# One ring of seven score banks in place of three pairs, in a four-block attention and expert kernel

## The chip, the core and the metric

The kernel runs as one program on one core of a Trainium2 chip. The metric is the device time of one execution in microseconds. PE is TensorE's matmuls, PEld its weight loads, DVE VectorE, ACT ScalarE, POOL GpSimd, SP SyncE. PSUM has eight banks of 512 fp32 values a partition, and it is the memory that matmuls write and that DVE and ACT read.

## The reference, cut to what matters

```python
# x: 4 x 512 x 256, context: 4 x 1601 x 256
x = x + tanh(g_xattn[0]) * xattn0(layernorm(x), context)   # block 1: 16 heads of 64, softmax over 1601 keys, Wo
x = x + tanh(g_ffn[0]) * ffn0(layernorm(x))                # block 2: below
x = x + tanh(g_xattn[1]) * xattn1(context, context, layernorm(x), mask)   # block 3: 16 heads of 16, 1601 masked keys, w_out
x = x + tanh(g_ffn[1]) * ffn1(layernorm(x))                # block 4: below

def ffn0(x):      # block 2
    src = rmsnorm(x + gqa(x))               # 16 query heads of 16, 4 key heads, 512 keys
    return rmsnorm(src + moe(src))          # 8 experts, 2 for each token, at most 640 tokens an expert

def ffn1(x):      # block 4
    attn = attention(x)                     # 16 heads of 16, 512 keys
    return attn + sum(combine[e] * (x @ W[e] + b[e]) for e in range(8))   # the best two weights, softmax gate
```

## The kernel before, in words

**Units and order.** Python code plans the whole program as one list of units (`order`), and each engine issues its part of every unit in the order of that list, waiting on the counting semaphores of the others. A unit is a small step: a matmul group on PE and what reads its result on ACT, DVE or POOL. `build_order` (from line 332) has eight generators for the first half of the program and eight for the second. The strings `TURNS_1` and `TURNS_3` say, digit by digit, from which generator the next unit comes. `Pace` (from line 194) keeps estimated times for every unit while the list is made; it chooses which part of the PSUM ring a unit gets. The assignment is fixed before the program runs.

**PSUM.** `RING` is 3: the ring is three pairs of banks (six banks). The two other banks, `pv_a` and `pv_b`, hold sums of value products: `pv_a` for blocks 1 and 3, `pv_b` for blocks 2 and 4. Every unit that needs PSUM takes a whole pair, the small ones too. A tile of scores with four heads (`scoreb`) takes two pairs, one for each half.

**Block 1** (`wide_...`, generators 0 to 4 of the first half): for each of 4 batches and 8 pairs of heads it projects keys (`kproj`), queries (`qproj`) and values (`vproj`), takes row maxima of bf16 scores (`maxa`, 16 units, matmul L1149 and DVE reduce L1671), turns them into a row (`rowa`), makes 13 tiles of scores with the maxima subtracted (`scorea`, L1165 and L1168, exp on ACT L1450, sums on POOL L1554), multiplies by the values (`pva`, L1179), and ends in `suma` and `outa` (ACT copy L1463). **Block 2** (generators 5 to 7) runs beside it, batch by batch, one batch behind.

**Blocks 3 and 4** share the second half: generator 0 mixes expert rows back, 1 makes scores of block 3, 2 its value products, 3 its maxima, 4 to 7 the same and the experts for block 4. Block 3 has 4 batches x 4 groups of 4 heads; a group has 13 key tiles. Each score tile (`scoreb`, mask matmuls L1290, score matmuls L1294, two exps L1457) uses 32x32 tiles of PE: a head lies on 32 rows (a strip), and four column parts of a head run side by side. The maxima of a group (`max3`) are 32 units: 4 query tiles x 4 key chunks x 2 pairs of heads; each fills a pair with 401 columns for either head (L1246, eight matmuls) and DVE adds the mask and reduces each bank (L1699, two instructions). `pvb` is a value product of a tile (L1310), and `tailb` (ACT copy L1467) ends a group. In block 4 `projqk` makes queries and keys of a group (L1214, L1215), `v4` the values (L1232, L1233), `expert4` one expert's product (L1388, L1389, DVE L1933).

**How a score tile waits.** In the code before, the two halves are issued one after the other, and the second waits for its own pair:

```python
for first in (0, 2):
    if first:
        for lane, other in plan.second_free[unit]:
            past.wait_ge(*at(lane, *other))
    ...   # masks of heads first, first + 1, then their scores
    last.then_inc(tensor_done, 1)
```

**Norms.** `ln`, `rms1` and `rms2` are one unit each: DVE makes means of squares, ACT takes the root (L1407), and DVE waits for it and then scales (L1653, L1835, L1852).

## Time and profile before

| | us |
|---|---|
| median of the runs | 3425.99 |
| lowest and highest of 3 | 3425.68, 3433.13 |
| the profiled execution | 3398.36 |
| its span, first to last instruction | 3396.6 |
| PE busy in the span | 3242.2 (95%) |
| DVE busy | 1980.8 (58%) |
| ACT busy | 1446.3 (43%) |
| POOL busy | 955.0 (28%) |
| mean granted clock of PE | 0.971 |

Busy means that at least one instruction of the engine runs. For PE a matmul on one 32x32 tile of the array counts as one on all of it. Rows of the trace name the line of the kernel, the engine, the operation and the tiles it writes and reads; the bracket behind a row tells how long the engine was idle before it and what ended that. "issue" stands for time in which the engine waited for nothing that the profile shows. The 27.6 us between the profiled execution and the median are part of what differs from execution to execution.

### The profile page before, as it was taken

To read this page: it belongs to the slowest core of one execution; us is meant where nothing else is said; L and a number is where in the kernel's file an instruction comes from. 1 tells how busy PE (TensorE), PEld (TensorE's weight loads), DVE (VectorE), ACT (ScalarE), POOL (GpSimd) and SP (SyncE) were. 2 spreads that over 40 slices of the span, in tenths; PEclk is the share of its full clock that TensorE was granted. 3 is DMA by queue.
4 is the path that set the end of the run, shared out by engine and by line. 5 is a ranking of instruction groups with operands and counts; after the bars stand their busy time and mean duration, and the time that the engine had idled before them with its cause. 6 is when DMAs were issued, how large, how long until landed. Compare 5 with 4: busy or idle time off the path is not lost.

```text
span 3396.6 us, 71446 instructions
## 1 busy us (share of the span) xinstructions
PE 3242.2 (95%) x30986; PEld 1431.6 (42%) x31007; DVE 1980.8 (58%) x4289; ACT 1446.3 (43%) x1645; POOL 955.0 (28%) x469
## 2 busy tenths in 40 slices
PE   7999999999999999999997979899999999999999
PEld 3444444444434444444433753223333334343344
DVE  4444456554655546565575028677777777766446
ACT  3444344445434453344433212355454454545533
POOL 4655554654465445555400000100000000000000
PEclk9999999999999999999988999899999999999989
DMA  4000000000000000000021622565343444443300
GB/s 152 12 13 13 28 12 15 7 11 33 7 21 12 13 28 7 21 12 12 4 116 39 188 81 75 132 175 158 97 120 115 127 124 117 118 118 113 115 26 20
DMA packets 85306, 221.17 MB, mean 65 GB/s; under 512 B 18424, under 2 KB 39168, under 8 KB 84224
## 3 DMA queue, kind: packets, MB, share of 16 engines
q1 hardware_dynamic: 79616, 201.65, 19.5%
q0 software_dynamic: 5376, 14.95, 2.0%
q8 instruction: 244, 4.00, 0.5%
q14 instruction: 70, 0.57, 0.1%
HBM read 204.61 MB, written 18.48 MB: 66 GB/s over the span
## 4 chain that ended last, share of the span: by engine, by line
PE 84%; DVE 6%; ACT 4%; POOL 3%; issue 1%; DMA 1%; ACTq 0%; POOLq 0%; DVEq 0%
PE ring L1294 13%; PE pv L1179 10%; PE ring L1168 9%; PE pv L1310 9%; PE ring L1246 3%; PE ring L1149 3%; PE ring L1140 3%; PE ring L1126 3%; PE ring L1141 3%; PE ring L1165 3%; PE ring L1127 2%; PE ring L1290 2%; POOL wide L1554 2%; PE ring L1367 2%; PE ring L1348 2%; PE ring L1260 2%
## 5 line engine op out<-in xcount | busy, mean ns | idle before, releaser
L1554 POOL TENSOR_TENSOR wide<-wide 124x1024 f32<-124x1024 f32 (+1 forms) x341 | 803.9, 2358 | 180.2 <-ACT wide L1450 142.2
L1457 ACT ACTIVATE wide<-ring 128x1024 f32<-128x1024 f32 (+1 forms) x544 | 536.2, 1023 | 498.4 <-PE ring L1294 494.6
L1671 DVE TENSOR_REDUCE max_a<-ring 128x2 f32<-128x802 f32 x512 | 493.4, 991 | 395.9 <-PE ring L1149 395.5
L1450 ACT ACTIVATE wide<-ring 124x1024 f32<-124x1024 f32 (+1 forms) x416 | 425.3, 1026 | 438.1 <-PE ring L1168 385.0
L1294 PE MATMUL ring<-slim 32*32 32x512 f32 (+1 forms) x7040 | 522.9, 607 | 0.3 <-DVE slim L1724 0.2
L1699 DVE CUSTOM_DVE_ANT_0 rest<-ring,slim 128x401 bf16<-128x401 f32 x683 | 374.9, 576 | 106.0 <-PE ring L1246 71.1
L1168 PE MATMUL ring<-wide 64*124 64x512 f32 (+1 forms) x1664 | 424.7, 588 | 0.0
L1179 PE MATMUL pv<-wide 124*64 124x512 f32 (+1 forms) x1664 | 413.9, 613 | 8.2 <-ACT wide L1450 8.2
L1709 DVE TENSOR_REDUCE slim<-ring 128x2 f32<-128x1024 f32 x256 | 308.0, 1222 | 111.9 <-PE ring L1260 105.4
L1524 POOL DMA_DIRECT2D slim<-in_ctx_k x16 | 8.9, 558 | 968.5 <-PE ring L1246 920.2
L1551 POOL TENSOR_TENSOR wide<-wide 124x1024 f32<-124x1024 f32 x31 | 73.1, 2357 | 599.5 <-ACT wide L1450 586.2
L1699 DVE CUSTOM_DVE_ANT_0 slim<-ring,slim 128x401 bf16<-128x401 f32 x341 | 195.8, 574 | 59.1 <-PE ring L1246 46.8
L1310 PE MATMUL pv<-wide,slim 128*17 128x512 f32 (+1 forms) x1664 | 226.4, 617 | 0.0
L1294 PEld LDWEIGHTS ring<-slim 32*32 32x32 f32 (+2 forms) x7040 | 173.3, 110 | 114.6 <-issue 73.8
L1246 PE MATMUL ring<-slim 32*32 32x401 bf16 x4096 | 192.0, 347 | 21.4 <-ACT wide L1457 8.8
L1179 PEld LDWEIGHTS pv<-wide 124*64 124x64 f32 (+1 forms) x1664 | 99.0, 136 | 229.2 <-issue 201.4
L1168 PEld LDWEIGHTS ring<-wide 64*124 64x124 f32 (+1 forms) x1664 | 155.5, 183 | 73.0 <-issue 50.4
L1246 PEld LDWEIGHTS ring<-slim 32*32 32x32 bf16 x4096 | 59.8, 88 | 288.6 <-ACT wide L1457 152.1
L1165 PE MATMUL ring<-wide,select_b 64*128 64x512 bf16 x832 | 159.0, 379 | 8.1 <-ACT wide L1450 6.1
L1149 PE MATMUL ring<-wide 64*128 64x401 bf16 x1024 | 155.5, 337 | 9.7 <-DVE max_a L1671 4.7
L1290 PE MATMUL ring<-slim,ident_b 32*32 32x512 bf16 (+1 forms) x3264 | 154.0, 394 | 10.9 <-ACT wide L1457 8.2
L1140 PE MATMUL ring<-wide 128*124 128x128 f32 (+1 forms) x832 | 162.1, 276 | 0.4 <-DVE max_a L1671 0.4
(238 smaller groups left out, 3964.3 us busy)
## 6 DMA issues: line engine op xcount, KB each, us to landing
slim<-masks SPq DMA_DIRECT2D x832, 128.0 KB, 2.7
slim<-in_ctx_k SPq DMA_DIRECT2D x16, 800.5 KB, 4.6
wide<-in_w_pair SPq DMA_DIRECT2D x32, 384.0 KB, 3.0
wide<-in_w SPq DMA_DIRECT2D x16, 512.0 KB, 4.7
wide<-in_we SPq DMA_DIRECT2D x16, 512.0 KB, 3.7
slim<-in_ctx_v SPq DMA_DIRECT2D x16, 442.0 KB, 5.9
wide<-in_ctxT SPq DMA_DIRECT2D x4, 1601.0 KB, 6.8
slim<-in_ctx_k POOLq DMA_DIRECT2D x16, 400.2 KB, 4.8
```

The lines of the kernel that those rows point to most:

```text
L1140: pe.matmul(place, ctxT[:, 0, k0:k0 + kn], pair_weights(p)[:, 2, 0, :], start=True, stop=False)
L1168: last = pe.matmul(slot[0:kn, h * BANK:(h + 1) * BANK], keys_a[own, p % 2, k0:k0 + kn], queries_a[own, p % 2, :], start=False, stop=True)
L1179: last = pe.matmul(pv_a[64 * h:64 * h + 64, :], values_a[0:kn, p % 2, k, 64 * h:64 * h + 64], exps_a[0:kn, slot_of["scorea", b, p, k], h * ...
L1246: last = pe.matmul(slot[j * PAD:(j + 1) * PAD, i * BANK:i * BANK + CHUNK], queries_low(3, g)[own, q * P + j * PAD:q * P + (j + 1) * PAD], ...
L1294: last = pe.matmul(head_bank(unit, h)[c0:c0 + cn, :], key_columns(blk, g, k0)[own, c0:c0 + cn], queries_place(blk, g)[own, :], start=blk ! ...
L1310: last = pe.matmul(pv_of[blk][PAD * h:PAD * h + rows_h, :], value_columns(blk, g, k, kn, h), exps_tile(blk, b, g, k, h)[0:kn, :], start=k ...
L1450: sc.activation(exps_a[0:kn, slot_of[unit], :], slot[0:kn, :], ACT.Exp, scale=WIDE ** -0.5).then_inc(scalar_done, 1)
L1457: sc.activation((exps_2 if blk == 2 else exps_34)[0:kn, first + 2 * i:first + 2 * i + 2, :].rearrange("p h n -> p (h n)"), ring_t[0:kn, ba ...
L1554: po.tensor_tensor(sums[0:kn, :], sums[0:kn, :], view, ALU.add).then_inc(pool_done, 1)
L1671: ve.reduce_max(max_a[:, :, q, c], slot.rearrange("p (h n) -> p h n", h=2)[:, :, 0:CHUNK], AX.X).then_inc(vector_done, 1)
L1699: ve.tensor_tensor_reduce(out=max_junk[junk], in0=slot[:, i * BANK:i * BANK + CHUNK], in1=maskQ_sb[:, q, CTX_CHUNKS[c]:CTX_CHUNKS[c] + CHUNK],
L1709: ve.tensor_reduce(neg_cols[blk][:, q, 2 * hp * PAD:2 * hp * PAD + PAD + 1:PAD], slot.rearrange("p (h n) -> p h n", h=2), AX.X, ALU.max, n ...
```

## The change

- The ring is seven single banks (`RING = 7`), and only `pv_a` keeps a bank of its own. Units whose result fits in one bank (`qproj`, `rowa`, `suma`, `projk`, `v2`, `strip`, `low`, `rowb`, `gate2`, `ranks`, `gate4`, `turn_comb`) take one. Units of a pair take banks 0 and 1, 2 and 3, or 4 and 5; bank 6 is for single ones alone.
- A score tile with four heads takes two pairs and waits for all four banks at its start. All masks are issued first, then all scores; ACT is told after head 1 and after head 3.
- `max3` has 64 units of one head and one bank, four matmuls and one DVE instruction, in place of 32 of two. The mask that DVE adds is laid out by chunk, with 1604 columns in place of 1601.
- The value sums of blocks 2 and 4 take one bank of the ring from the first value tile of a group to its copy on ACT.
- `projqk`, `v4` and `expert4` are two units of one bank each.
- `ln`, `rms1` and `rms2` are split: `stats` or `squares` (DVE, then the root on ACT) and the scaling as a unit of its own, which can lie further on in the order. Each has its own place for the root.
- `Pace` keeps a time for each of PE's four strips of rows and for the issue, and both strings of turns are new: 3911 turns in place of 3323.

```diff
-RING = 3
+RING = 7
+        if step.slots in (2, 4):
+            pairs = sorted(range(0, RING - 1, 2), key=lambda i: max(self.ring[i:i + 2]))[:step.slots // 2]
+            self.picked = tuple(bank for i in pairs for bank in (i, i + 1))
+        elif step.slots == 1:
+            ready = [i for i in range(RING) if self.ring[i] <= at]
+            self.picked = (max(ready, key=lambda i: self.ring[i ^ 1] if i ^ 1 < RING else 1e9) if ready else min(range(RING), key=lambda i: self.ring[i]),)
...
-                for c in range(len(CTX_CHUNKS)):
-                    for hp in range(2):
-                        yield Step(0.17 if b or g else 0.8, (("ve", 1.12),), 1, (("low", b, g),), ("max3", b, g, q, hp, c),
+                for c, h in product(range(len(CTX_CHUNKS)), range(GROUP)):
+                    yield Step(0.18 if b or g else 0.5, (("ve", 0.525),), 1, (("low", b, g),), ("max3", b, g, q, h, c),
...
-            yield Step(3.5, (("ve", 1.7),), 1, (("bias4", b),), ("expert4", b, e))
+            for i in range(2):
+                yield Step(1.75, (("ve", 0.85),), 1, (("bias4", b),), ("expert4", b, e, i))
...
-        ring_t = ctx.enter_context(nc.psum_tensor("ring", [P, RING, 2 * BANK], F32))
-        pv_t = ctx.enter_context(nc.psum_tensor("pv", [P, 2, BANK], F32))
-        pv_a, pv_b = pv_t[:, 0, :], pv_t[:, 1, :]
+        ring_t = ctx.enter_context(nc.psum_tensor("ring", [P, RING, BANK], F32))
+        pv_a = ctx.enter_context(nc.psum_tensor("pv", [P, BANK], F32))[:, :]
...
-                    for first in (0, 2):
-                        if first:
-                            for lane, other in plan.second_free[unit]:
-                                past.wait_ge(*at(lane, *other))
-                        if blk == 3:
-                            for h, (c0, cn) in product(range(first, first + 2), parts):
...
+                    if blk == 3:
+                        for h, (c0, cn) in product(range(GROUP), parts):
+                            own = slice(PAD * h, PAD * h + cn)
+                            pe.matmul(ring_t[c0:c0 + cn, bank_of[unit][h], :], ident_b[own, own],
+                                      mask_places[n % MASK_PLACES][own, c0 // PAD, :], start=True, stop=False)
+                    for h, (c0, cn) in product(range(GROUP), parts):
+                        own = slice(PAD * h, PAD * (h + 1))
+                        last = pe.matmul(ring_t[c0:c0 + cn, bank_of[unit][h], :], key_columns(blk, g, k0)[own, c0:c0 + cn],
+                                         queries_place(blk, g)[own, :], start=blk != 3, stop=True)
+                        if h == 1 and c0 == parts[-1][0]:
+                            last.then_inc(tensor_done, 1)
+                    last.then_inc(tensor_done, 1)
...
-                if kind in ("ln", "rms1", "rms2"):
-                    past.wait_ge(vector_done, plan.end["vector", unit] - {"ln": QT, "rms1": QT, "rms2": 2 * QT}[kind])
-                    sc.activation(rstd[:, :], rstd[:, :], ACT.Sqrt).then_inc(scalar_done, 1)
+                if kind in ("stats", "squares"):
+                    past.wait_ge(*at("vector", *unit))
+                    sc.activation(root_of(unit), root_of(unit), ACT.Sqrt).then_inc(scalar_done, 1)
```

## Rows read from the trace of the kernel before

**Rows 1.** Table by stage: stretch; length, busy us of each engine; clock, DMA share, GB/s.

```profile
core 0: us, PE busy (x) PEld busy (x) DVE busy (x) ACT busy (x) POOL busy (x), PEclk, DMA share, GB/s
355.00:1730.00 1375.00, 1341.27 (x7515) 610.94 (x7514) 764.69 (x1037) 603.91 (x706) 698.52 (x306) 0.99 0.05 15
1730.00:1835.00 105.00, 93.12 (x477) 35.23 (x483) 69.82 (x138) 42.79 (x49) 7.71 (x8) 0.89 0.24 95
1835.00:2010.00 175.00, 158.74 (x709) 123.52 (x710) 27.86 (x67) 36.70 (x53) 8.81 (x10) 0.94 0.45 140
2010.00:2120.00 110.00, 85.22 (x1134) 29.42 (x1143) 81.42 (x291) 23.76 (x26) 15.88 (x17) 0.91 0.28 73
2120.00:3260.00 1140.00, 1105.59 (x18173) 411.63 (x18156) 785.47 (x2400) 560.05 (x598) 22.74 (x30) 0.97 0.44 122
3260.00:3396.60 136.60, 121.76 (x1199) 62.75 (x1201) 84.33 (x139) 41.13 (x49) 0.00 (x0) 0.93 0.06 20
```

**Rows 2.** Timeline, one cycle of block 3: start, length in us, engine, line, operation.

```profile
2280.76 0.40 PE L1290 MATMUL ring<-slim,ident_b 32*32 32x512 bf16 x8
...
2283.28 0.11 PEld L1246 LDWEIGHTS ring<-slim 32*32 32x32 bf16 x8 [0.68 <-ACT wide L1457]
2283.30 0.58 DVE L1699 CUSTOM_DVE_ANT_0 rest<-ring,slim 128x401 bf16<-128x401 f32 x1 [0.98 <-PE ring L1246]
...
2284.58 0.41 PE L1290 MATMUL ring<-slim,ident_b 32*32 32x512 bf16 x8
...
2284.81 1.04 PE L1294 MATMUL ring<-slim 32*32 32x512 f32 x16
...
2285.29 0.57 DVE L1699 CUSTOM_DVE_ANT_0 slim<-ring,slim 128x401 bf16<-128x401 f32 x1
2285.43 0.11 PEld L1290 LDWEIGHTS ring<-slim,ident_b 32*32 32x32 bf16 x8 [0.49 <-DVE max_b L1699]
...
2285.79 0.57 DVE L1699 CUSTOM_DVE_ANT_0 rest<-ring,slim 128x401 bf16<-128x401 f32 x1
2286.04 1.95 ACT L1457 ACTIVATE wide<-ring 128x1024 f32<-128x1024 f32 x2 [1.89 <-PE ring L1294]
...
2287.07 0.58 DVE L1699 CUSTOM_DVE_ANT_0 rest<-ring,slim 128x401 bf16<-128x401 f32 x1 [0.70 <-PE ring L1294]
...
2287.41 0.13 PEld L1310 LDWEIGHTS pv<-wide,slim 128*17 128x17 f32 x8 [0.18 <-issue]
2287.41 1.05 PE L1310 MATMUL pv<-wide,slim 128*17 128x512 f32 x8
...
2288.57 0.40 PE L1290 MATMUL ring<-slim,ident_b 32*32 32x512 bf16 x8
```

**Rows 3.** Timeline: a score tile of block 4 whose four banks were free.

```profile
2513.34 1.15 PE L1294 MATMUL ring<-wide 32*32 32x512 f32 x32
...
2514.54 1.94 ACT L1457 ACTIVATE wide<-ring 128x1024 f32<-128x1024 f32 x2 [1.40 <-PE ring L1294]
```

**Rows 4.** What ended PE's idle time before L1246 (two rows), L1290 (two rows).

```profile
  ACT wide L1457: 149.9, 202
  DVE max_b L1699: 67.0, 92
...
  DVE max_b L1699: 87.4, 152
  ACT wide L1457: 32.2, 37
```

**Rows 5.** Who waited for ACT's root L1407: us in total, times.

```profile
  DVE src L1653: 8.9, 8
  DVE src L1852: 7.5, 4
  DVE slim L1653: 5.6, 4
  DVE wide L1653: 4.3, 4
```

**Rows 6.** Timeline: ACT's copies that end a wide pair (L1463), a masked group (L1467).

```profile
123.98 0.60 ACT L1463 ACTIVATE raw_a<-pv 128x512 f32<-128x512 f32 x1 [1.87 <-PE pv L1179]
169.99 0.60 ACT L1463 ACTIVATE raw_a<-pv 128x512 f32<-128x512 f32 x1 [1.85 <-PE pv L1179]
...
2213.79 0.60 ACT L1467 ACTIVATE raw_a<-pv 128x512 f32<-128x512 f32 x1 [1.91 <-PE pv L1310]
2268.25 0.60 ACT L1467 ACTIVATE raw_a<-pv 128x512 f32<-128x512 f32 x1 [1.67 <-PE pv L1310]
2321.13 0.60 ACT L1467 ACTIVATE raw_a<-pv 128x512 f32<-128x512 f32 x1 [2.12 <-PE pv L1310]
```

**Rows 7.** The chain of work: two fp32 matmuls of an expert unit, start and length.

```profile
3258.24 0.43 PE ring L1389 x2
```

More of the change, by code:

```diff
@@ L44 @@
 DIVIDE = 0.13
+ISSUE = 0.05
 AHEAD = 0.5
@@ L180, with __init__ @@
+    "33533323133613325333653321771462412146212147442214741214217525656162521617226444474467447644774477447744457546"
+    "454645464446744457546454645464446744454474565464546447465756565766776"
 )
 class Step:
-    def __init__(self, pe=0.0, use=(), slots=0, needs=(), name=None, parts=(1, 1), first=None, second=0.0, mark=None, late=0.0):
+    def __init__(self, pe=0.0, use=(), slots=0, needs=(), name=None, parts=(1, 1), mark=None, late=0.0, rows=range(4), hold=0):
         self.pe, self.use, self.slots, self.needs, self.name = pe, use, slots, needs, name
-        self.parts, self.first, self.second, self.mark, self.late = parts, first, second, mark, late
+        self.parts, self.mark, self.late, self.rows, self.hold = parts, mark, late, tuple(rows), hold
@@ L208, in accept @@
+        at = max([at] + [self.ring[i] for i in self.picked])
         end = at
         if step.pe:
-            turned = self.pe + (DIVIDE if step.parts[0] != self.parts else 0.0)
-            at = max(at, turned)
-            if self.spare and at - self.pe >= WARM_FROM:
-                self.spare(at - self.pe)
-            end = at + step.pe
-            if step.slots == 2:
-                end += max(0.0, self.ring[self.picked[1]] - at - step.second)
-            self.pe, self.parts = end, step.parts[1]
+            if step.parts[0] != self.parts:
+                free = max(self.busy) + DIVIDE
+            else:
+                free = max(self.busy[r] for r in step.rows)
+            if self.spare and at - max(self.busy) >= WARM_FROM:
+                self.spare(at - max(self.busy))
+            self.issued = at + ISSUE
+            end = max(at, free) + step.pe
+            for r in range(4):
+                self.busy[r] = end if r in step.rows else max(self.busy[r], end - step.pe) if step.parts[0] != self.parts else self.busy[r]
+            self.pe, self.parts = max(self.busy), step.parts[1]
@@ L229, in accept @@
+            last = self.lane[lane] = max(self.lane[lane], ready) + time
+            if i == 0 or (i == 1 and step.slots == 4):
+                for bank in self.picked[2 * i:] if step.slots == 4 else self.picked:
+                    self.ring[bank] = last + HOP
+                if step.hold == 2:
+                    self.ring[self.held] = last + HOP
             if step.mark is None or i <= step.mark:
@@ L232, in accept @@
             for i in self.picked:
-                self.ring[i] = end + HOP
+                self.ring[i] = 1e9 if step.hold else end + HOP
+                self.held = i
         if step.name:
@@ L538, in slim_values @@
             also = (("outb", 3, b - 1),) if blk == 3 and b and last and g == 0 else (("bias4", b),) if blk == 4 and last else ()
[L539 to L541 removed]
+            own = blk != 3
+            yield Step(0.88, (("sc", 0.6), ("ve", 2.25 if g % 2 else 1.55)) if last else (), int(own and k == 0),
+                       (("scoreb", blk, b, g, k),) + valued + also, unit, (-4, -4), hold=int(own and k == 0) + 2 * int(own and last))
+            if own and k == 0:
+                in_slot(unit, "none")
+                bank, = plan.bank[unit]
+            emit(on(unit, *(() if own else pv_left)))
             expo.free[plan.slot["scoreb", blk, b, g, k]] = (("tensor", unit),)
```

429 lines of the change are left out of this document (221 added, 208 removed).

## The prediction

> **What bounds the kernel now.** I read the table by stage first [rows 1]. It cuts the span of 3396.6 us in seven: the wide attention (0 to about 1730), what is left of the grouped attention (to 1835), the expert layer (to 2010), the gathers (to 2120), a long stage in which masked attention and the last layer run together (2120 to 3260), and a tail. PE looks full everywhere: 1341 of 1375 us in the wide stage, 1106 of 1140 in the long one. In the wide stage this is nearly true work: of one pair of heads the copies of the sums stand 46.0 us apart [rows 6], and PE's idle time there is 33.7 us in 1375. In the long stage it is not, because a matmul on one 32-row strip counts as a busy PE though three other strips stand still. So I read one cycle of masked attention in the timeline [rows 2].
>
> There a score tile (`scoreb`) is issued in two halves. Masks and scores of heads 0 and 1 start at 2284.58, those of heads 2 and 3 at 2285.43, after a wait for DVE to leave the second pair of banks. Each half streams for 1.04 us on two strips only. Both exps follow in one run of 1.95 us from 2286.04. DVE takes six maxima, 0.50 us from start to start, and then stands still for 0.70 to 0.98 us until PE has new ones, which have no bank: the one pair left of the three is DVE's own, and PE's weight load waits until ACT has read another. The starts of three score tiles, 2280.76, 2284.58 and 2288.57, give a cycle of 3.9 us. DVE's work in it is 6 x 0.50 = 3.0 us, ACT's 1.95. PE's, if all four strips ran together as they do in a tile whose banks are all free (1.15 us, [rows 3]), would be 1.15 + 0.2 of masks + 1.05 of values + three double maxima of at most 0.17 stream each, about 2.9. Nobody is full; the three pairs of banks couple them. The waits by line say it for the stage [rows 4]: maxima wait for ACT's banks 149.9 us and for DVE's 67.0; masks wait for DVE's 87.4 and ACT's 32.2. Much of this lies under matmuls still running, so it is a sign and not a sum. The stage as a whole: DVE 785 and ACT 560 of 1140 us.
>
> **The change, part by part.** All on the profiled execution (3398.4 us with 1.8 around its span); the median of the runs is 3426.0, 27.6 above it, and I add that at the end.
>
> *Seven single banks; one-bank maxima; four-bank scores.* The masked maxima become 1024 units of one bank instead of 512 of a pair. Matmuls, reduce instructions and bytes stay the same; what is added is a wait and a signal for each, which costs nothing I can see, since DVE's two instructions of a unit already follow each other at the same 0.50 us as those of different units [rows 2]. A score tile takes two pairs and lets nothing start before all four banks are free. While it is in flight DVE has three banks, not two, and a bank comes back after each reduce. Work out the cycle: at 0 the masks start; the exps begin 1.46 later (2284.58 to 2286.04), say 1.5 with 16 mask loads ahead; they last 1.95; the bank goes over within 0.1. So the late pair of a score is free at 3.5. The next score can take that late pair and the pair it did not use, if the maxima in between sit in the single bank and in the early pair (free at 2.5). DVE needs 3.0 of these 3.5 us, PE 2.9. The cycle is then 3.5 instead of 3.9, bound by the two exps behind one score. There are 13 x 16 = 208 such tiles: 208 x 0.4 = 83 us. Against it: the accumulators of blocks 2 and 4 lose their own bank and hold one of the seven from the first value tile to the tail. With one bank gone the ring is three pairs again, and the cycle 3.9, as now. Block 4 holds one through much of the last three quarters of the stage. I take 60 of the 83; the bounds are 30 and 83. A check from other rows: with no block 4 beside it a group takes 54.5 and 52.9 us [rows 6]; 13 x 3.9 is 50.7 of that, so 13 x 3.5 makes it 48 to 49, and the same 8 to 10% on 1140 is 90 to 110. The bound is not reached there, as two engines would be at 80%; this leaves room below 60, not a forecast.
>
> *Splitting.* `projqk`, `v4` and `expert4` become two units each: 16 + 4 + 32 = 52 more. An expert unit is eight pairs of matmuls at 0.43 us, 3.4 us [rows 7], during which DVE has at most the work of the one pair in hand, about 1 us. Halved, PE can feed DVE in between. Per block this is worth from 0 to 1 us, 0 to 52 in all; I take 20, as DVE is behind in about a third of the stage. It is paid for by changes of PE's tile shape: the first weights of a value tile wait 0.18 us on "issue" after 32-row work [rows 2]. If each of the 52 extra units stands alone between masked work, that is two changes each, 52 x 2 x 0.18 = 19 us; I take 8. Net -12, from +19 to -52.
>
> On that change of shape TensorEngine Tiling (the Trainium skill, Key Properties) says that a change of tiling mode drains the engine while tiles within a mode run independently. The trace agrees with 0.18 us beside it. Taken in full the rule speaks against finer units, since a drain behind a score is its whole 1.15 us; by it the 52 units would cost up to 52 x 1.15 = 60 us, not 8.
>
> *Norms in two units.* The root of ACT comes between two DVE units, so DVE can go on instead of waiting for it. These waits are 8.9 + 7.5 + 5.6 + 4.3 us in the whole kernel [rows 5], 26.3; half of them lie where DVE is short. I take -8, from 0 to -26. The roots and the table loads stay as many. A split norm can also come later on its chain, which only the ends of stages would feel (up to 3 us each).
>
> *The wide stage.* Its tiles keep their pairs, and it is PE's own work that fills it. Smaller units (query projection, row sums, the single-bank steps of block 2) now leave the pairs alone. At most PE's 33.7 idle us and the staggered halves of block 2's 64 scores are to be had; those now need two free pairs at once, between wide scores that want them too. I take -15, from +15 to -50.
>
> *Ends.* Expert layer and gathers keep pairs, weights and DMAs: 0, within 3. The mask rows grow from 1601 to 1604 columns, nothing. In the tail (PE 121.8 of 136.6 us, [rows 1]) smaller expert units help DVE a little: -5, from +2 to -10.
>
> Sum: -60 - 12 - 8 - 15 - 5 = -100. 3398.4 - 100 = 3298; with the 27.6, **3326 us**.
>
> **Rivals.** *A, the wait moves ahead of the whole score.* Today the masks of the second half wait 119.6 us for DVE and ACT [rows 4] while the first half streams. The new code waits for all four banks first, so if the order leaves maxima in the banks that the score needs, the first exp comes that much later: 119.6 / 208 = 0.57 us on a cycle of 3.9, and the maxima behind it leave DVE empty for longer, so nothing gives it back. That is +120 us in the long stage and, by its measure, some +15 in block 2's 64 scores: with the other gains of 40, +80 to +95, about 3510. It decides from the point at which a score waits for DVE in over half of its cycles. For it speaks that DVE begins a run of maxima at 2287.07, only 1.5 us before the next score [rows 2]; against it, that two of three pairs can be had without DVE by 3.5 us.
>
> *B, the gain is larger.* If the uncoupled stage gets PE or DVE near 85%, the 1140 us fall to DVE's 785 / 0.85 = 924, or, with the value and projection work that PE cannot share, to some 1000: -140 there, with the rest -180, about 3245.
>
> *C, it cancels.* Held banks keep the cycle at 3.9 for most of the stage and the shape changes eat the splitting: -20 or so, 3406, and up to 3436 if the wide stage loses its 15.
>
> *D, PE's clock.* The granted clock is 0.97 in the long stage, almost all at the level of 2.4 GHz, and 0.89 to 0.94 in the stages with gaps, more of them at 1.2 GHz [rows 1]. New gaps would move the long one there: 3% of PE's 1106 is 33 us back. It only shrinks the gain to about 3359, inside my own range.
>
> **Chances.** Forecast (with D) 0.60, own range 3283 to 3385; B 0.16; C 0.13; A 0.11. The range takes in most of B and the better half of C: 3228 to 3416; it leaves out A, the other half of C (0.06) and the far end of B (0.03), 0.20 in all. A measurement tells about 0.3% here, 10 us, so "same" is 3416 to 3436. Faster: 0.60 + 0.16 + 0.07 of C = 0.83; same 0.06; slower 0.11, all but A's chance.
>
> **What would show it.** The cycle of the masked scores in the timeline: 3.5 us where block 4 holds no bank; all 16 masks ahead of the 16 scores, and one run of two exps behind each. Masked groups with nothing beside them 48 to 49 us apart, not 53 to 54. The waits of the masks for DVE gone or under 40 us; if they are over 120 and the groups are 58 us apart, A is right. In the wide stage pairs of heads still 46 us apart, and its end 10 to 20 us earlier. DVE's waits for the root near 0. The number of "issue" waits ahead of 128-row weights shows the price of the shape changes. I am wrong in kind if the long stage keeps its 1140 us, or if the wide stage moves more than it.

## The result, and the profile after

The kernel after takes 3319.47 us, median of 4 runs (3317.64 to 3320.65), against 3426.70 us for the kernel before run beside it (4 runs, 3425.68 to 3433.13). The ratio is 0.968, with an interval of 0.967 to 0.970. The forecast was 3326. The profiled executions are 78.1 us apart in their spans, 3396.6 and 3318.5, and not 107: the kernel before was profiled in one of its quicker executions. Where the time went is read from these two.

The first view is the list of ACT's copies that end a stage. In the kernel before, the last wide copy, the first masked one and the last masked one:

```profile
1723.51 0.60 ACT L1463 ACTIVATE raw_a<-pv 128x512 f32<-128x512 f32 x1 [1.64 <-PE pv L1179]
...
2142.71 0.60 ACT L1467 ACTIVATE raw_a<-pv 128x512 f32<-128x512 f32 x1 [1.86 <-PE pv L1310]
...
3256.86 0.60 ACT L1467 ACTIVATE raw_a<-pv 128x512 f32<-128x512 f32 x1 [0.84 <-PE pv L1310]
```

The same in the kernel after, with the next three masked ones ([rows 6] has those of before):

```profile
1728.41 0.60 ACT L1506 ACTIVATE raw_a<-pv 128x512 f32<-128x512 f32 x1 [1.70 <-PE pv L1225]
...
2163.31 0.60 ACT L1510 ACTIVATE raw_a<-pv 128x512 f32<-128x512 f32 x1 [2.02 <-PE pv L1352]
2213.61 0.60 ACT L1510 ACTIVATE raw_a<-pv 128x512 f32<-128x512 f32 x1 [2.77 <-DVE max_b L1742]
2276.84 0.60 ACT L1510 ACTIVATE raw_a<-pv 128x512 f32<-128x512 f32 x1 [2.73 <-PE pv L1352]
2329.71 0.60 ACT L1510 ACTIVATE raw_a<-pv 128x512 f32<-128x512 f32 x1 [1.40 <-PE pv L1352]
...
3187.25 0.60 ACT L1510 ACTIVATE raw_a<-pv 128x512 f32<-128x512 f32 x1 [1.98 <-PE pv L1352]
```

Subtract stage by stage. The wide attention ends 4.9 us later. From there to the first masked copy it is 434.9 us where it was 419.2, 15.7 more. From the first masked copy to the last it is 1023.9 where it was 1114.2, **90.3 less**. From there to the end of the span it is 131.3 where it was 139.7, 8.4 less. Sum: +4.9 +15.7 -90.3 -8.4 = -78.1. The long stage alone gains more than the whole kernel.

The table by stage of the kernel after answers [rows 1]; the columns are the same:

```profile
355.00:1730.00 1375.00, 1330.06 (x7506) 608.30 (x7502) 797.74 (x1058) 606.98 (x711) 703.68 (x308) 0.99 0.05 15
1730.00:1835.00 105.00, 88.84 (x487) 30.68 (x485) 68.56 (x120) 40.72 (x46) 8.07 (x8) 0.90 0.24 94
1835.00:2010.00 175.00, 153.86 (x692) 119.33 (x692) 29.02 (x74) 37.63 (x54) 8.81 (x10) 0.94 0.44 136
2010.00:2120.00 110.00, 80.55 (x839) 30.01 (x843) 68.02 (x245) 11.18 (x13) 15.86 (x17) 0.81 0.19 54
2120.00:3190.00 1070.00, 987.50 (x18527) 417.94 (x18511) 798.06 (x2458) 563.81 (x611) 23.09 (x30) 0.98 0.47 133
3190.00:3318.50 128.50, 116.19 (x1178) 59.45 (x1178) 81.31 (x133) 42.22 (x49) 0.00 (x0) 0.94 0.06 18
```

In the long stage PE's busy time fell by 118 us with no work taken away: when four strips run at once instead of two, the same matmuls cover less time. DVE's 798 us now fill 75% of the stage, before 69%. The clock did not fall (0.98, before 0.97). In the gathers it did, to 0.81 from 0.91; a standstill comes ahead of that fall (see the paragraph on expert layer and gathers below).

One cycle of block 3 in the timeline answers [rows 2]. All six maxima that DVE starts in it are shown:

```profile
2289.66 0.44 PE L1330 MATMUL ring<-slim,ident_b 32*32 32x512 bf16 x16 [0.26 <-ACT wide L1500]
...
2289.88 1.35 PE L1334 MATMUL ring<-slim 32*32 32x512 f32 x32
...
2289.93 0.57 DVE L1742 CUSTOM_DVE_ANT_0 rest<-ring,slim 128x401 bf16<-128x401 f32 x1
...
2290.43 0.57 DVE L1742 CUSTOM_DVE_ANT_0 rest<-ring,slim 128x401 bf16<-128x401 f32 x1
...
2291.10 1.94 ACT L1500 ACTIVATE wide<-ring 128x1024 f32<-128x1024 f32 x2 [1.70 <-PE ring L1334]
...
2291.32 0.58 DVE L1742 CUSTOM_DVE_ANT_0 slim<-ring,slim 128x401 bf16<-128x401 f32 x1 [0.32 <-PE ring L1290]
...
2291.82 0.57 DVE L1742 CUSTOM_DVE_ANT_0 rest<-ring,slim 128x401 bf16<-128x401 f32 x1
...
2292.32 0.57 DVE L1742 CUSTOM_DVE_ANT_0 rest<-ring,slim 128x401 bf16<-128x401 f32 x1
...
2292.81 0.57 DVE L1742 CUSTOM_DVE_ANT_0 slim<-ring,slim 128x401 bf16<-128x401 f32 x1
...
2293.30 0.44 PE L1330 MATMUL ring<-slim,ident_b 32*32 32x512 bf16 x16 [0.60 <-ACT wide L1500]
```

All 16 masks stand ahead of the scores, the scores stream for 1.35 us, both exps follow in one run 1.44 us after the masks began, and the next masks start 0.26 us after that run ends: 3.64 us. DVE takes two maxima while the scores stream, as their banks are not the score's, and stands still for 0.32 us only.

One cycle can mislead, so I took the starts of the masks of all consecutive tiles of block 3 from the timelines, and counted how many maxima DVE began between two of them:

| kernel | 6 or 7 maxima: tiles, median us | 2 or 3 maxima: tiles, median us | tiles under 4 us | mean of all, us |
|---|---|---|---|---|
| before | 38, 4.93 | 57, 3.69 | 85 | 5.64 |
| after | 38, 3.64 | 40, 3.53 | 104 | 5.30 |

The shortest cycles hardly changed. What changed is what fits into one: six maxima made a cycle of 4.93 us before and fit into a short one now. They are not the only ones. Cycles with no maximum or one fell as well, from 4.91 us (31 tiles) to 3.64 (43), those with four or five from 4.17 (41) to 3.92 (50); those with eight or more stayed, 7.94 (40) and 7.97 (36).

What ended PE's idle time before the masks (L1330, two rows) and, in the long stage, before the maxima (L1290, three rows), in answer to [rows 4], then who waited for ACT's root (L1449, two rows), in answer to [rows 5]; us in total, times:

```profile
  DVE max_b L1742: 73.6, 97
  ACT wide L1500: 69.4, 86
...
  DVE max_b L1742: 124.9, 199
  issue: 80.6, 240
  ACT wide L1500: 28.7, 48
...
  DVE wide L1697: 6.0, 2
  DVE src L1882: 2.9, 2
```

The maxima no longer wait for ACT (149.9 us, now 28.7) but more for DVE (67.0, now 124.9), which is the fuller engine. The masks' waits did not go away: 119.6 us before, 143.0 now. "Issue" waits ahead of the maxima rose from 20.3 us (44 times) to 80.6, and those ahead of the scores fell from 64.1 us (200 times) to 13.1 (25). Such sums take in the idle time of the weight loads, most of it under matmuls that still run: PE itself idles for only 34 us of the long stage before and for 83 us after (length less busy time, in the table by stage).

### The profile page after: what moved, and what is told of

Same layout as the page of the kernel before. It is cut to its first block, busy times and chain, and to the rows that moved or that the text cites. A ratio compares the mean times of both kernels' runs of the same rounds, so it can differ in the third digit from the quotient of the medians.

```text
span 3318.5 us, 72188 instructions
## 1 busy us (share of the span) xinstructions
PE 3093.5 (93%) x31006; PEld 1427.6 (43%) x31006; DVE 2008.8 (61%) x4293; ACT 1437.8 (43%) x1645; POOL 955.3 (29%) x469
## 4 chain that ended last, share of the span: by engine, by line
PE 77%; DVE 10%; ACT 5%; issue 4%; POOL 2%; DMA 1%; another core or an unknown queue 1%; DVEq 0%; ACTq 0%; POOLq 0%
PE ring L1334 10%; PE pv L1225 10%; PE ring L1214 9%; ACT wide L1500 4%; PE pv L1352 3%; PE ring L1195 3%; PE ring L1172 3%; PE ring L1211 3%; PE ring L1173 3%; PE ring L1352 3%; PE ring L1186 3%; PE ring L1187 2%; PE ring L1290 2%; PE ring L1330 2%; PE ring L1390 2%
## 5 line engine op out<-in xcount | busy, mean ns | idle before, releaser
L1500 ACT ACTIVATE wide<-ring 128x1024 f32<-128x1024 f32 (+1 forms) x544 | 527.5, 1020 | 447.0 <-PE ring L1334 427.7
L1225 PE MATMUL pv<-wide 124*64 124x512 f32 (+1 forms) x1664 | 404.6, 607 | 3.9 <-ACT wide L1492 3.9
L1334 PE MATMUL ring<-slim 32*32 32x512 f32 (+1 forms) x7040 | 370.0, 616 | 14.5 <-DVE max_a L1715 6.5
L1290 PE MATMUL ring<-slim 32*32 32x401 bf16 x4096 | 216.8, 344 | 27.6 <-DVE max_b L1742 15.4
L1352 PE MATMUL pv<-wide,slim 128*17 128x512 f32 (+1 forms) x1664 | 226.2, 617 | 0.9 <-ACT wide L1500 0.8
L1290 PEld LDWEIGHTS ring<-slim 32*32 32x32 bf16 x4096 | 89.9, 88 | 297.2 <-DVE max_b L1742 147.6
L1334 PEld LDWEIGHTS ring<-slim 32*32 32x32 f32 (+2 forms) x7040 | 138.1, 110 | 71.1 <-issue 27.9
L1500 ACT ACTIVATE slim<-ring 128x1024 f32<-128x1024 f32 x128 | 124.1, 1021 | 95.4 <-PE ring L1334 93.7
```

The lines of the kernel that those rows point to most:

```text
L1225: last = pe.matmul(pv_a[64 * h:64 * h + 64, :], values_a[0:kn, p % 2, k, 64 * h:64 * h + 64], exps_a[0:kn, slot_of["scorea", b, p, k], h * ...
L1290: last = pe.matmul(slot[j * PAD:(j + 1) * PAD, 0:CHUNK], queries_low(3, g)[own, q * P + j * PAD:q * P + (j + 1) * PAD], keys_low(3, g)[own ...
L1334: last = pe.matmul(ring_t[c0:c0 + cn, bank_of[unit][h], :], key_columns(blk, g, k0)[own, c0:c0 + cn], queries_place(blk, g)[own, :], start ...
L1352: last = pe.matmul(pv_tile(blk, b, g)[PAD * h:PAD * h + rows_h, :], value_columns(blk, g, k, kn, h), exps_tile(blk, b, g, k, h)[0:kn, :], ...
L1500: sc.activation((exps_2 if blk == 2 else exps_34)[0:kn, first + 2 * i:first + 2 * i + 2, :].rearrange("p h n -> p (h n)"), ring_t[0:kn, ba ...
```

## The experiments

The kernels ran in three groups, each with the kernel before beside it. That kernel took 3399.28 us in the first (the four runs that come first), 3423.01 us in the second and 3399.74 us in the third, so a kernel is compared with others of its own group, or by its ratio to the kernel before. The kernel after ran in the second group, at 3319.38 us and ratio 0.970 (0.969 to 0.972). It did not run in the first and the third, so what stands against it from there is given by plain times and by ratios.

### The new units with the old order

```diff
-TURNS_1, TURNS_3 = (the strings of after)
+TURNS_1, TURNS_3 = (the strings of before)
+    def halved(name):
+        return name and (name[0] in ("stats", "squares") or name[0] == "max3" and name[4] % 2 == 0 or
+                         name[0] in ("projqk", "v4", "expert4") and name[-1] == 0)
...
+        more = True
+        while more:
+            more = halved(steps[n].name)
+            pace.accept(steps[n])
+            steps[n] = next(streams[n], None)
```

Banks and units are those of after. Where the old order had one unit, both halves are issued one behind the other.

> The changed kernel with its seven banks, one-bank maxima, split units and four-bank score tiles, but emitted in the order of the kernel before: each unit of before is replaced on the spot by the one or two units that do its work. Theory 1 (banks and units carry the gain, the order only fits them): at least half of the 107 us stays, 3340 to 3375 us. Theory 2 (the new order carries it): no gain is left, 3415 to 3440 us. Theory 3 (they only work together, since a score tile now waits for four banks in an order that was made for two): slower than before, 3450 to 3520 us, with the masks' waits for DVE in the masked stage above 150 us.

Measured: 3559.03 us, ratio 1.045 (1.040 to 1.049), so 4.5% slower than the kernel before. Long stage in the table by stage, then what ended PE's idle time before the masks (L1333 here):

```profile
2120.00:3416.00 1296.00, 1062.57 (x18190) 420.54 (x18190) 791.52 (x2410) 549.06 (x595) 22.69 (x30) 0.89 0.38 108
```
```profile
  DVE max_b L1745: 118.4, 111
  ACT wide L1503: 91.3, 84
  issue: 71.3, 65
```

The stage takes 1296 us where it took 1140. A cycle with six or seven maxima takes 5.69 us in the median (47 tiles) where before took 4.93. PE's granted clock is 0.89 where it was 0.97, more of the stage at 1.2 GHz, and PE is busy for 82% of the stage where it was busy for 97%. Theory 3 is right in kind only: the time lies 39 us above its range, and the masks' waits for DVE, to be above 150 us, are 118.4. Waits for DVE and ACT of 209.7 us ahead of the masks, where the kernel after has 143.0, and longer cycles fit rival A. What the waits, the order and the clock each cost is not separated.

### The old banks with the new order

```diff
-TURNS_1, TURNS_3 = (the strings of before)
+TURNS_1, TURNS_3 = (the strings of after)
+    def doubled(name):
+        return name and name[0] in ("ln", "rms1", "rms2", "max3", "projqk", "v4", "expert4")
...
+        if doubled(steps[n].name) and n not in waiting:
+            waiting.add(n)
+            continue
+        waiting.discard(n)
```

This is the kernel before (the diff stands against it), with its order taken from the new strings: where they name two halves, its one unit is issued at the turn of the second.

> The kernel before with its three pairs, double maxima, joined norms and whole expert units, but emitted in the new order (a unit of before stands where the second of its two new units stands). Theory 1 (banks and units): 3420 us or more, since the order cannot give maxima a third bank. Theory 2 (order): 3330 to 3360 us. Theory 3 (both together): slower than before, 3450 us or more.

Measured: 3564.66 us, ratio 1.048 (1.045 to 1.051). That is theory 3 in kind, and theory 1 allowed it too (3420 or more). Neither half of the change is worth anything alone: the new order is not a better one for the old banks, and the new banks lose with the old order.

### The score in halves again

```diff
+                    for first in (0, 2):
+                        if first:
+                            for lane, other in plan.second_free[unit]:
+                                past.wait_ge(*at(lane, *other))
...
-                    for h, (c0, cn) in product(range(GROUP), parts):
+                        for h, (c0, cn) in product(range(first, first + 2), parts):
```

Banks, units and order of after; masks and scores of heads 2 and 3 wait for their own pair and come behind those of heads 0 and 1, as in the kernel before.

> The changed kernel in which only the way a score tile is issued goes back: masks and scores of heads 0 and 1 as soon as the first pair of banks is free, then those of heads 2 and 3 after a wait for the second pair. Order and banks stay. If all four strips at once are what shortened the cycle, the masked cycle grows from 3.6 to about 4.2 us and the kernel is 40 to 100 us slower (3360 to 3420). If the wait for all four banks ahead of the tile costs more than the strips give (the mechanism of rival A), it is faster: up to 0.5 us on 208 tiles, 3220 to 3310. If a tile is bound by its two exps in either form, within 10 us of 3319.

Measured: 3376.18 us, ratio 0.994 (0.991 to 0.997), against 0.970 with whole scores. In spans it is 3371.2 against 3314.3 and 3318.5, 53 to 57 us, and by the ratios 80 to 87 us. One tile in the timeline:

```profile
2492.43 0.50 PE L1335 MATMUL ring<-slim,ident_b 32*32 32x512 bf16 x16 [0.43 <-DVE max_b L1745]
...
2492.65 1.69 PE L1339 MATMUL ring<-slim 32*32 32x512 f32 x29
...
2493.87 1.96 ACT L1503 ACTIVATE wide<-ring 128x1024 f32<-128x1024 f32 x2 [2.27 <-PE ring L1339]
2494.15 0.62 PE L1339 MATMUL ring<-slim 32*32 32x512 f32 x3
...
2494.86 0.58 DVE L1745 CUSTOM_DVE_ANT_0 rest<-ring,slim 128x401 bf16<-128x401 f32 x1 [1.05 <-PE ring L1339]
...
2496.55 0.50 PE L1335 MATMUL ring<-slim,ident_b 32*32 32x512 bf16 x16 [0.32 <-DVE max_b L1745]
```

Here all four banks were free, and still the tile takes from 2492.43 to 2494.77, 2.34 us, where the whole tile takes from 2289.66 to 2291.23, 1.57. The first exp starts 1.44 us after the masks in both. What is lost is the second half's time, which PE cannot give to the maxima: DVE stands still for 1.05 us where it did for 0.32. Cycles with six or seven maxima take 4.22 us in the median (40 tiles) where after took 3.64, and 40 tiles are under 4 us where 104 were. So with the order kept, issuing all masks and then all scores is worth 50 to 90 us. That order was made for whole scores; halves with an order of their own were not run, and what follows on such prices makes this an upper end.

### The maxima in pairs again, order kept

```diff
-                for c, h in product(range(len(CTX_CHUNKS)), range(GROUP)):
-                    yield Step(0.18 if b or g else 0.5, (("ve", 0.525),), 1, (("low", b, g),), ("max3", b, g, q, h, c),
+                for c in range(len(CTX_CHUNKS)):
+                    for hp in range(2):
+                        yield Step(0.18 if b or g else 0.8, (("ve", 1.05),), 2, (("low", b, g),), ("max3", b, g, q, hp, c),
```

Only the maxima take a pair for two heads; of two turns that named single ones the second is used.

> The changed kernel with the maxima of the masked block as units of two heads and a pair of banks again, each where its second half stood; everything else is new. If one-bank units are the core of the change, the masked stage goes back most of the way: a pair can only be the one that no score holds, 3380 to 3440 us. If the order and the four-strip tiles carry the gain, within 15 us of 3319. My theory of the cycle says about 3390.

Measured: 3398.72 us, ratio 1.000 (0.998 to 1.003). By the ratios that is 103 us over after, by the plain times 79. The whole gain is gone, with the order kept.

### The kernel after, once more

It ran a second time, unchanged, to stand in one group with the next three.

> The changed kernel as it is, to have it beside the others: the kernel before took 3426.7 us beside it at first and 3399.3 beside the first four experiments. If the before kernel's time differs between chips and the changed one's doesn't, 3319 us again and a ratio near 0.976; if both scale, 3293 us and 0.968.

Measured: 3319.38 us (3316.08 to 3324.51), as in the first run. The kernel before took 3423.01 beside it, not 3399, so the two cases that were named were not told apart. Cycles with six or seven maxima: 3.64 us again.

### Six ring banks, order kept

```diff
-RING = 7
+RING = 6
...
-            own = blk != 3
+            own = False
...
-            return pv_a if blk == 3 else slot_tile(("pvb", blk, b, g, 0))
+            return pv_a if blk == 3 else pv_b
```

The value sums of blocks 2 and 4 have their own bank again, and the ring six.

> The changed kernel without the seventh ring bank: six single banks, and blocks 2 and 4 have their own bank for value sums again. Units and order stay; the planner only places them anew in six banks. If the third bank for maxima during a score tile is what counts, the masked stage loses much of its gain: 3360 to 3400 us. If a single bank that is now and then held is worth little and one-bank units in a pair are what counts, within 15 us of the changed kernel.

Measured: 3695.21 us, ratio 1.081 (1.078 to 1.084), 376 us over after in the same group, where 3360 to 3400 us were expected. The mean granted clock is 0.931, after has 0.973. Cycles with six or seven maxima take 7.63 us.

### Whole projection and expert units, order kept

```diff
-            for i in range(2):
-                yield Step(1.75, (("sc", 0.65), ("ve", 0.45)), 1,
+            yield Step(3.5, (("sc", 1.3), ("ve", 0.9)), 2,
...
-            for i in range(2):
-                yield Step(1.75, (("ve", 0.85),), 1, (("bias4", b),), ("expert4", b, e, i))
+            yield Step(3.5, (("ve", 1.7),), 2, (("bias4", b),), ("expert4", b, e))
```

`projqk`, `v4` and `expert4` are one unit of a pair each, as in the kernel before.

> The changed kernel with projqk, v4 and expert4 as one unit of a pair of banks each, standing where their second halves stood. My prediction gave the split 12 us net, from -19 to +52: 3331 us, from 3300 to 3371. Rival: order and units are fitted so closely that undoing any of it costs far more than the part is worth, over 60 us, 3380 or more, as undoing the order did.

Measured: 3480.44 us, ratio 1.016 (1.014 to 1.018), 161 us over after. That is outside the prediction's 3300 to 3371 and what the rival named, 3380 or more.

### Norms in one unit, order kept

```diff
-        emit(("squares", 1, b))
...
-        emit(("rms1", b))
+        emit(("squares", 1, b), ("rms1", b))
```

The same for `ln` and `rms2`: DVE waits for the root where it made the squares.

> The changed kernel with every norm's two DVE units standing together again, at the place of the second, so that DVE waits for the root. Banks are the same. My prediction gave the split 8 us, from 0 to 26: 3327 us. Rival: DVE's stalls lie where PE waits for it with full banks, and each of 24 costs PE over 1.5 us: 3355 us or more.

Measured: 3347.74 us, ratio 0.978 (0.976 to 0.980), 28.4 us over after. The largest entry under who waited for the root (L1445 here):

```profile
  DVE src L1894: 13.9, 4
```

DVE's waits for the root are 26 us in all; the kernel after has 10. The time lies between the 3327 of the prediction and the 3355 of its rival. Several of these kernels lose more than the whole change gained, by taking away one piece of it. That is a result about the order and not about the piece. So I found the order anew for the main pieces.

### The order fitted again, and three pieces taken away with a fitted order

The four kernels below have strings of turns of their own. Each was found in the same way: start from the turns of the kernel before, move single turns, keep a move when the planner's own estimate (`Pace`) falls. The search is no exhaustive one, and it need not have been equally lucky in all four; differences of 10 us between them mean little. The first has all parts of the change.

```diff
-TURNS_1, TURNS_3 = (the strings of after)
+TURNS_1, TURNS_3 = (strings found from those of before)
```

> The control for the next three. Banks, units and waits of the changed kernel; only the order is another: found by moving single turns of the order, starting from the order of the kernel before (the 3559 us of the first experiment), with the planner's own estimate to judge them. If what the kernel needs is an order that is fitted to its banks, whichever it is, it returns to 3319 us or a little above it, 3320 to 3345. If the changed order has something that such a search doesn't see, it stays above 3380.

Measured: 3281.82 us (3278.98 to 3285.47), ratio 0.965 (0.962 to 0.968), lower than either expectation. It is the best kernel found; against after it was not run side by side, and the intervals of the ratios, 0.962 to 0.968 and 0.967 to 0.970, just touch. By the plain times it is 38 us quicker, by the ratios 11 to 18. By the spans the masked attention ends at 3141.57, 46 us earlier than in after:

```profile
2010.00:2120.00 110.00, 82.76 (x1208) 31.36 (x1214) 82.97 (x302) 23.48 (x26) 15.85 (x17) 0.91 0.28 75
2120.00:3142.00 1022.00, 948.49 (x18074) 408.27 (x18066) 775.96 (x2390) 547.51 (x595) 23.05 (x30) 0.98 0.49 136
```

29 of the 46 us are had before the first masked copy, at 2134.51 where after has 2163.31: the gathers run at clock 0.91 again. Banks and units are the same in both, so what after lost there belongs to its order.

Six banks, with an order of its own (edit as above):

> Six ring banks and a bank of their own for the value sums of blocks 2 and 4, everything else new, with an order found for it in the same way and time as the control's. Theory 1 (the third bank for maxima during a score tile is the core of the change): 60 to 100 us over the control, and no gain or little over the kernel before. Theory 2 (the 376 us of the experiment with six banks came from its unfitted order): within 30 us of the control.

Measured: 3381.12 us, ratio 0.993 (0.991 to 0.996), 99.3 us over the fitted kernel with seven. Its masked attention ends at 3244.97, 103.4 later; 10.5 of them are lost before its first masked copy (2144.98) and 92.9 from there on, so nearly all of it lies in the long stage. One cycle:

```profile
2241.26 0.44 PE L1330 MATMUL ring<-slim,ident_b 32*32 32x512 bf16 x16
...
2242.70 1.94 ACT L1500 ACTIVATE wide<-ring 128x1024 f32<-128x1024 f32 x2 [0.78 <-PE ring L1334]
2243.72 0.17 PEld L1290 LDWEIGHTS ring<-slim 32*32 32x32 bf16 x12 [1.07 <-DVE max_b L1742]
...
2245.05 0.11 PEld L1290 LDWEIGHTS ring<-slim 32*32 32x32 bf16 x8 [0.85 <-DVE max_b L1742]
...
2245.95 0.44 PE L1330 MATMUL ring<-slim,ident_b 32*32 32x512 bf16 x16 [0.54 <-DVE max_b L1742]
```

With two banks left beside the score, PE can lay up two maxima and must then wait for DVE before each further step, 1.07 and 0.85 us. The exps end at 2244.64, but the next masks come at 2245.95, after 4.69 us. Cycles with six or seven maxima take 4.88 us in the median (42 tiles), as in the kernel before, where after takes 3.64 and the fitted one with seven banks 3.65 (56 tiles).

Whole projections and experts, with an order of their own:

> The changed kernel with projqk, v4 and expert4 as whole units of a pair of banks, with an order found for it in the same way. My prediction's price for the split, 12 us from -19 to 52, means 12 us over the control. Theory 2 (PE's blocks of 3.4 us starve DVE each time): 30 to 60 us over it. The 161 us of the same kernel with the order unfitted would then be mostly the order's.

Measured: 3315.11 us, ratio 0.975 (0.972 to 0.978), 33.3 us over the fitted kernel: in the range that theory 2 named, 30 to 60. It lies in the long stage: masked attention ends at 3172.38, 30.8 later, though its first copy comes 4.8 us earlier.

Maxima in pairs, with an order of their own:

> The changed kernel with maxima as units of two heads and a pair of banks, with an order found for it in the same way. If one-bank maxima are the core, over 50 us above the control; if their 79 us with the order unfitted were the order's, under 20 us above it.

Measured: 3323.43 us, ratio 0.976 (0.973 to 0.980), 41.6 us over the fitted kernel, between the two theories. Cycles with six or seven maxima take 5.05 us (53 tiles).

Put side by side, the price of taking a piece away:

| piece | order kept, us over after | order fitted, us over the fitted kernel |
|---|---|---|
| seventh bank | 376 | 99 |
| projections and experts in halves | 161 | 33 |
| maxima of one bank | 79 to 103 | 42 |

With the order kept, each piece looks two to five times as dear as with a fitted one. PE takes its units strictly in turn, so one unit that waits for a bank holds up all that stand behind it, also those whose banks are free. The three fitted prices make 174 us, and all that the fitted kernel gains over the kernel before is 118, so they overlap. It may be that the seventh bank is of little use if the maxima come in pairs, and the other way round; no run takes both away. The old banks and units with an order found anew were not run either, so how much of the 118 us is the search's own is open. The prices in the table do not hang on that, as both sides of each have a fitted order.

## Why the prediction was right, point by point

**The sum.** On the profiled execution -100 was forecast and -78 came. The median came out at 3319 against 3326 only because the 27.6 us that were added to the profiled time found no counterpart in the kernel after, whose eight spans lie at 3314.3 to 3322.3 in both of its groups. So it is luck that the total is only 7 us off: 22 us too much gain and 27.6 us too much on top cancel. The terms are worth more than the total.

**The long stage, -60 and -12 and most of -8, forecast -80; came -90.** The mechanism was right: seven banks let DVE work beside a score. The six-bank kernel with a fitted order shows it, since it loses 99 of 118 us and its cycles with six or seven maxima go back to those of the kernel before, 4.88 and 4.93 us. The price of the cycle was read wrongly. I took 3.9 us as the usual cycle, from one group in the timeline [rows 2], and 3.5 as the new floor. Counted over all tiles, the short cycles were 3.72 us in the median before (those of 3 to 4.5 us) and are 3.64 now, so the floor moved by 0.08 and not by 0.4. The cycles with six or seven maxima, 38 in either kernel, fell from 4.93 to 3.64: 38 x 1.29 = 49 us. The cycle in [rows 2] was itself one with six maxima and shorter than most such. The term was nearly right in size, as 208 x 0.4 = 83 cut to 60 stands for what is 38 x 1.3 and something from cycles with fewer maxima. That the size came out is therefore partly luck. The held bank, for which I took off 23 us, shows in no row that I found.

**The groups.** Pure masked groups were to be 48 to 49 us apart. They are 50.3, 63.2 and 52.9 us, where the kernel before had 71.1, 54.5 and 52.9 between the same copies (2142.71, then [rows 6]). That forecast failed for this kernel. It laid the shorter cycle over all 13 tiles of a group, and it did not foresee the standstills that the part on the gathers shows; the 63.2 us hold two of them. In the fitted order, which has none, the same distances are 51.8, 49.8 and 54.3. The gain sits later, where block 4 runs beside the scores: from 2329.71 to 3187.25 it is 857.5 us, in the kernel before from 2321.13 to 3256.86 it was 935.7.

**The masks' waits, forecast under 40 us for DVE; are 73.6.** They stand where the theory of rival A put them, 143.0 / 208 = 0.69 us ahead of each whole score, more than the 0.57 I had computed for A, and the kernel is still faster. So the sum of such waits is no measure of lateness. Nor is the time from the masks to the first exp, whose median over all tiles is 1.45 us before, 1.44 after and 1.44 with the old order, where the kernel is slower: A's wait lies ahead of the masks. What speaks against A here is the cycle itself, 5.30 us in the mean where it was 5.64.

**Splitting, forecast -12 net, 20 of gain and 8 of shape changes.** Its fitted worth is 33 us, inside -52 to +19 and nearly three times the value I took. I had credited it with DVE being fed during a 3.4 us expert unit in a third of the stage. The price was about as small as forecast. "Issue" waits of the weight loads in the long stage, ahead of the first weights of value products (L1310, now L1352) and of the expert's first matmul (L1388, now L1430), before and then after:

```profile
  issue: 84.8, 250
...
  issue: 3.4, 8
```
```profile
  issue: 72.1, 244
...
  issue: 12.0, 35
```

The experts pay 8.6 us more, the value products 12.7 less: together -4 us. The 60 us that would follow if each of the 52 units cost the time of a whole score are not there. One reason is their number: the weight loads change between 128 and 32 rows 607 times in the long stage before and 645 times after, 38 more, where I had counted 104 at most. TensorEngine Tiling (the Trainium skill, Key Properties) states the drain. This trace agrees that there is one: at a change the load of the new weights starts only 0.07 us before the last matmul's end as the profile models it (in the median), at other times 0.4 us before it. The load has idled for 0.34 us by then (84.8 / 250, 12.0 / 35), but under matmuls that still ran: the "issue" waits in these rows are those of weight loads, and none is a matmul's.

**Norms, forecast -8, 0 to -26.** DVE's waits for the root fell from 27.4 us (the 26.3 of the prediction and 1.1 ahead of L1835, which it left out) to 10.4, not quite to the near 0 that was said. Joined again with the order kept they cost 28.4 us, but after what the table above shows of such numbers that is an upper end. A fitted order without the split was not tried.

**The wide stage, forecast -15, came +4.9.** Pairs of heads are still 46 us apart, which was right, and the range (+15 to -50) held it. The step that failed is the belief that smaller units would give PE its 33.7 idle us: PE now idles for 44.9 (1375 less 1330.06). The fitted kernel ends this stage at 1728.24 too, and there PE idles for 30.9 us. So the stage takes its time whether PE idles 31 or 45 us. With the new banks and the old order it ends at 1720.23, 3.3 us earlier than in the kernel before, so single banks bring it little, and the 5 us come with the orders; what in them does it was not found.

**Expert layer and gathers, forecast 0 within 3, came +15.7.** This is the one term that missed its own range. Up to the first masked score nothing is lost: its masks start at 2085.53, before at 2080.59, 4.9 us later as at the end of the wide stage. All 15.7 us come between them and the first masked copy, and 10.9 of them in one cycle: the next masks follow after 14.8 us, before after 3.9. In it DVE stands still for 9.34 us, ACT for 4.67 and PE for 7.49. The profile names "remote" as what ended DVE's and ACT's wait, which means an event that it ties to no instruction. The granted clock is 1.00 from 2080 to 2087 and falls after PE has stopped, as the first two rows show (clock behind POOL's busy time). Scores that take 1.35 us at the higher clock then take 2.27:

```profile
2087.00:2097.00 10.00, 2.16 (x35) 0.49 (x25) 1.48 (x5) 2.05 (x2) 5.33 (x6) 0.73 0.40 122
2097.00:2120.00 23.00, 19.42 (x328) 5.60 (x330) 16.42 (x67) 5.81 (x6) 0.00 (x0) 0.60 0.31 88
...
2095.52 0.58 DVE L1742 CUSTOM_DVE_ANT_0 rest<-ring,slim 128x401 bf16<-128x401 f32 x1 [9.34 <-remote]
...
2096.16 1.02 PE L1290 MATMUL ring<-slim 32*32 32x401 bf16 x16 [7.49 <-DVE max_b L1742]
...
2100.74 2.27 PE L1334 MATMUL ring<-slim 32*32 32x512 f32 x32
```

I had looked for changes of code in this stage, found none, and wrote 0. But the order changed, and that is enough: 839 matmuls stand in the window where 1134 stood. The fitted order has 1208 in it, the clock at 0.91, and loses nothing. The standstill comes back in the second run of the kernel after (DVE 9.5 us) and in the kernels with six banks, whole units and joined norms, which keep its order; with halves or paired maxima in that order, in the kernel before and in the four fitted ones there is none. In the group that takes 63.2 us ACT waits in the same way twice, 5.57 us up to 2256.75 and 3.29 up to 2261.07. What holds the engines there is open.

**The tail, forecast -5, came -8.4.** Within its range.

**The rivals.** B (3245) was nearer to what the change can do than to what this version does: the fitted order reaches 3282 beside 3400, ratio 0.965, and DVE's 776 us are 76% of its long stage, not 85%. C did not happen. The first experiment looks like A, the kernel does not. D did not happen in the long stage, but the gathers, where the forecast had nothing to lose, ran at 0.81, behind a standstill of PE, DVE and ACT.

## What to carry to other kernels

When engines take their work in a fixed order, a change of buffers and the order belong together: measure a piece of such a change only with an order found for it, or its price is mostly that of the misfit (376 us against 99 for the seventh bank). Ask of a buffer ring what the fuller engine can do while the largest user holds its share, and count that over all cycles, sorted by the work in them, not in one that happens to be on the screen. And a stage whose code is untouched is not a stage whose order is untouched.

## What the runs showed of the hardware

- The kernel before took 3399.3, 3423.0 and 3399.7 us in three groups of runs, medians that repeat within a group, and 3426.7 us in the first comparison though its own profiled execution took 3398.4. The kernel after took 3319.5 and 3319.4 us in the two where the kernel before took about 3425, so its ratio may be up to 0.976 where the other takes 3399 (3319 / 3399). It was not run there. The level goes with the granted clock: 0.970 to 0.972 in the executions of the kernel before that took under 3405 us, 0.966 to 0.969 in those of 3416 to 3428. The three groups ran on three chips. What sets the two levels is open.
- 16 masks and 32 scores issued across four strips at once take 1.57 us. The same work issued as two strips and then the other two takes 2.34 us, with all banks free. Both are read from one tile; maxima run in the free strips meanwhile.
- PE's granted clock was 0.97 to 0.98 in the long stages in which PE is busy for 92% or more, and 0.89 in the one in which it is busy for 82% (1062.57 of 1296). In the gathers it was 0.81 with PE busy for 73% and 0.91 with 75%; the first has a standstill of 7.49 us, with the clock at 0.60 in the 23 us behind it.
- At a change between 32-row and 128-row weights the new load starts 0.07 us before the last matmul's modelled end, in the median of the long stage before and after; among loads of one shape it starts 0.4 us before it.
